# A two-attention block on one Trainium2 core: scores lead by 19 instead of 21, later projections, and instruction lists written anew

## The reference, cut to what matters

```python
# 1: attention with 16 heads of 16; only the 307 rows with the largest
#    sparsity = max(scores) - mean(scores) keep their output, others give zero
scores = einsum('bhqd,bhkd->bhqk', q, k) * scale
sparsity = scores.max(-1) - scores.mean(-1)
_, top_idx = top_k(sparsity, U)                # U = 307 of 512, per head
out_sel = einsum('bhuk,bhkd->bhud', softmax(scores of top_idx), v)
x = x + out.at[..., top_idx].set(out_sel) @ Wo + bo
x = x + ffn(layernorm(x))     # 2: 256 -> 1024 -> 256, 4 of 16 blocks of 64 kept per row by a router
x = x + gla(layernorm(x))     # 3: gated linear attention over the batch axis (8 steps), then a silu ffn
x = x + ffn(layernorm(x))     # 4: the same weights as 2
```

## Time and profile before

| what | value |
|---|---|
| median of 3 runs | 1562.42 us (1561.67 to 1566.0) |
| the profiled execution | 1563.17 us |
| its span | 1561.4 us |
| granted PE clock, mean over the span | 0.977 of full speed |
| front, before unit 0's first T | 0 to 56.4 us |
| 16 units of attention, to the mask | 56.4 to 526 us |
| START | about 530 to 951 us |
| MERGED, then CLOSE | 951 to 1409, then to 1561 us |

### The profile page before, as it was taken

How to read it: one execution, slowest core, us unless ns; L and a number is a source line. 1 busy time by engine, 2 the same in 40 slices (tenths; PEclk the granted TensorE clock), 3 DMA queues, 4 the chain that set the end, 5 groups by cost and what they waited for, 6 DMA issues and landing times.

```text
span 1561.4 us, 25522 instructions
## 1 busy us (share of the span) xinstructions
PE 1473.3 (94%) x8840; PEld 1049.0 (67%) x8840; DVE 1111.0 (71%) x2127; ACT 664.9 (43%) x971; POOL 557.6 (36%) x705
## 2 busy tenths in 40 slices
...
DMA packets 56414, 61.04 MB, mean 39 GB/s; under 512 B 15733, under 2 KB 41637, under 8 KB 56349
## 3 DMA queue, kind: packets, MB, share of 16 engines
...
## 4 chain that ended last, share of the span: by engine, by line
PE 53%; issue 19%; DVE 13%; POOL 8%; ACT 4%; SPq 1%; DMA 1%; POOLq 0%; ACTq 0%; DVEq 0%
PE ps L1961 15%; PE ps L1989 10%; PE ps L958 5%; PE ps L943 4%; PE ps L929 4%; PE ps L886 3%; POOL h L1564 3%; DVE mc L630 2%; PE ps L1972 2%; POOL kT L1537 2%; PE ps L1947 2%; PE ps L896 1%; PE ps L2001 1%; DVE race L729 1%; DVE top L728 1%
## 5 line engine op out<-in xcount | busy, mean ns | idle before, releaser
L630 DVE TENSOR_REDUCE mc<-ps 128x2 f32<-128x1024 f32 x256 | 305.5, 1220 | 46.2 <-PE ps L929 45.7
L1989 PE MATMUL ps<-w_hi,h 128*128 128x256 f32 x1024 | 220.7, 299 | 6.0 <-DVE h L1801 6.0
L1868 ACT ACTIVATE h<-ps 128x512 fp32r<-128x512 f32 x128 | 75.8, 597 | 314.0 <-PE ps L2019 314.0
L1801 DVE SCALAR_TENSOR_TENSOR h<-ps,h 128x512 fp32r<-128x512 f32 x128 | 87.6, 690 | 128.7 <-ACT h L1868 126.0
L346 POOL DMA_DIRECT2D k_st<-k_hi x256 | 124.1, 491 | 152.7 <-PE ps L943 75.3
L1989 PEld LDWEIGHTS ps<-w_hi,h 128*128 128x128 f32 x1024 | 166.9, 190 | 13.7 <-DVE h L1801 11.2
L1961 PE MATMUL ps<-xT_b,w_hi 128*128 128x512 f32 x512 | 166.8, 407 | 0.0
L1564 POOL TENSOR_TENSOR h<-hf,h 128x512 fp32r<-128x512 f32 x56 | 72.5, 1294 | 250.5 <-DVE h L1814 250.5
L1989 PE MATMUL ps<-w_lo,h 128*128 128x256 f32 x512 | 143.9, 281 | 0.0
L943 PE MATMUL ps<-q_st,k_st 64*128 64x512 f32 x512 | 122.7, 478 | 16.6 <-ACT pT1b L816 5.0
L1537 POOL TENSOR_TENSOR kT<-kT,aT 128x128 f32<-128x128 f32 (+6 forms) x56 | 72.0, 1286 | 156.4 <-DVE pr L1728 106.6
...
## 6 DMA issues: line engine op xcount, KB each, us to landing
q_st<-q_hi SPq DMA_DIRECT2D x256, 32.0 KB, 2.1
k_st<-k_hi POOLq DMA_DIRECT2D x256, 32.0 KB, 1.9
q_st<-q_lo SPq DMA_DIRECT2D x128, 32.0 KB, 2.0
k_st<-k_lo POOLq DMA_DIRECT2D x128, 32.0 KB, 1.9
...
```

Of the source, the lines that this page charges most:

```text
L630: v.tensor_reduce(mc[par][:, qt, 2 * HU + j:MC:NPAIR], ps[:, at:at + 2, :], AX_X, ALU.max).then_inc(max_done, 1)
L1801: v.scalar_tensor_tensor(lo[:, :], ps[:, RING[s] + m % 2, :], 0.0, hi[:, :].bitcast(F32), ALU.max, ALU.subtract).then_inc(F[s]["hl"], 1)
L1868: a.activation(h[s][m % 2][0][:, :], ps[:, RING[s] + m % 2, :], ACT.Relu).then_inc(F[s]["relu"], 1)
L1989: last = t_.matmul(ps[:, ACC[s] + t // 2, (t % 2) * D:(t % 2 + 1) * D], h[s][m % 2][a][:, t * P:(t + 1) * P], ws[k][:, m, :], start=m == 0 ...
```

## The change

`AHEAD` goes from 5 to 3: 16 + 3 = 19 scores are made before unit 0, S 0 to 12 of a unit belong to the next unit and S 13 to 15 to the one after. 14 hand-written lists of attention are written anew (those for units 0, odd, even and 14 on PE, ACT and DVE, for unit 15 on PE and ACT). POOL's once-only work goes behind even units only. `START`, `MERGED` and `CLOSE` are written anew. No instruction is added to any engine, and none is removed; they are moved.

```diff
-AHEAD = 5
+AHEAD = 3
 PE_UNITS (the odd and the even list, and the start of unit 14's)
-    "odd": [("S", 0), ("T", 0, 0), ("V0",), ("T", 0, 1), ("S", 1), ("AV", 0), ("T", 1, 0), ("S", 2), ("K", 0),
-        ("S", 3), ("T", 1, 1), ("AV", 1), ("S", 4), ("T", 2, 0), ("K", 1), ("S", 5), ("T", 2, 1), ("S", 6), ("AV", 2),
-        ("T", 3, 0), ("Q", 0), ("Q", 1), ("T", 3, 1), ("S", 7), ("AV", 3), ("S", 8), ("T", 4, 0), ("V1",),
-        ("T", 4, 1), ("S", 9), ("AV", 4), ("T", 5, 0), ("S", 10), ("O1",), ("S", 11), ("T", 5, 1), ("AV", 5), ("mx",),
-        ("T", 6, 0), ("S", 12), ("mean",), ("T", 6, 1), ("S", 13), ("AV", 6), ("T", 7, 0), ("S", 14), ("AV", 7),
-        ("T", 7, 1), ("S", 15), ("O0",)],
+    "odd": [("S", 0), ("S", 1), ("T", 0, 0), ("V0",), ("T", 0, 1), ("AV", 0), ("S", 2), ("S", 3), ("T", 1, 0),
+        ("K", 0), ("K", 1), ("S", 4), ("T", 1, 1), ("S", 5), ("AV", 1), ("T", 2, 0), ("AV", 2), ("S", 6), ("T", 2, 1),
+        ("Q", 0), ("S", 7), ("T", 3, 0), ("S", 8), ("Q", 1), ("S", 9), ("T", 3, 1), ("AV", 3), ("S", 10), ("T", 4, 0),
+        ("V1",), ("T", 4, 1), ("S", 11), ("AV", 4), ("T", 5, 0), ("S", 12), ("O1",), ("S", 13), ("T", 5, 1),
+        ("AV", 5), ("mx",), ("T", 6, 0), ("S", 14), ("AV", 6), ("T", 6, 1), ("mean",), ("S", 15), ("T", 7, 0),
+        ("AV", 7), ("O0",), ("T", 7, 1)],
-    "even": [("S", 0), ("T", 0, 0), ("X0",), ("AV", 0), ("T", 0, 1), ("X1",), ("S", 1), ("T", 1, 0), ("S", 2),
-        ("AV", 1), ("S", 3), ("T", 1, 1), ("K", 0), ("S", 4), ("T", 2, 0), ("K", 1), ("S", 5), ("T", 2, 1), ("AV", 2),
...
+    "even": [("S", 0), ("X0",), ("S", 1), ("T", 0, 0), ("S", 2), ("X1",), ("S", 3), ("T", 0, 1), ("S", 4), ("AV", 0),
+        ("T", 1, 0), ("S", 5), ("AV", 1), ("T", 1, 1), ("S", 6), ("K", 0), ("T", 2, 0), ("K", 1), ("S", 7),
+        ("T", 2, 1), ("S", 8), ("AV", 2), ("T", 3, 0), ("Q", 0), ("Q", 1), ("T", 3, 1), ("AV", 3), ("S", 9),
+        ("T", 4, 0), ("S", 10), ("AV", 4), ("T", 4, 1), ("S", 11), ("O1",), ("S", 12), ("T", 5, 0), ("T", 5, 1),
+        ("mx",), ("AV", 5), ("T", 6, 0), ("S", 13), ("mean",), ("T", 6, 1), ("S", 14), ("AV", 6), ("T", 7, 0),
+        ("S", 15), ("AV", 7), ("T", 7, 1), ("O0",)],
...
 DVE_UNITS (odd)
-    "odd": [("stats", 0), ("max", 0), ("V0",), ("max", 1), ("max", 2), ("stats", 1), ("max", 3), ("max", 4), ("K",),
...
+    "odd": [("stats", 0), ("max", 0), ("max", 1), ("stats", 1), ("V0",), ("max", 2), ("max", 3), ("max", 4),
...
 attention.pool, the loop over units
             unit(u)
-            if u < len(ffn_pieces):
-                ffn_low(u)
-            elif u < len(ffn_pieces) + 3:
-                spread(u - len(ffn_pieces))
-            elif u < len(ffn_pieces) + 6:
+            if u % 2 == 0 and u < 10:
+                ffn_low(u // 2)
+            if u in (2, 4, 6, 8):
+                eng.wait_ge(ffn_lo, u // 2 + 1)
+            if u in (2, 4, 6):
+                spread(u // 2 - 1)
+            if u in (8, 10, 12):
                 eng.wait_ge(v_moved, u // 2 + 1)
-                bias_part(u - len(ffn_pieces) - 3)
+                bias_part((u - 8) // 2)
```

In even units DVE's `x_low` steps move from behind maxima 0 and 1 to behind maximum 4. In unit 14 the maxima are 0 to 12 where they were 0 to 10. In `START`, as PE sees it, the steps around the first two recurrences become:

```diff
-z.T f1.m1c f1.mk z.o0 z.o1 z.o2 og z.o3 z.o4 f1.m0 z.o5 z.o6 z.o7 z.o8 rec0 f1.m1 rec1 f1.d0 rec2 rec3 rec4 rec5 f1.m2 f1.d1 rec6 rec7
+z.T f1.rt z.o0 z.o1 z.o2 og z.o3 z.o4 z.o5 z.o6 z.o7 f1.m0c z.o8 rec0 f1.m1c f1.mk rec1 rec2 rec3 f1.m0 rec4 f1.m1 f1.d0 rec5 f1.m2 rec6 f1.d1 rec7
-g.u1 z.o7 z.o8 rec0 rec1 g.d0 rec2 rec3 rec4 g.m2 rec5 rec6 g.u2 g.d1 rec7 g.m3 g.u3 o.mean
+g.u1 z.o7 z.o8 g.d0 g.m2 rec0 rec1 g.u2 rec2 g.d1 rec3 rec4 g.m3 rec5 rec6 g.u3 g.d2 rec7 g.m4 g.u4 o.mean
```

More of the change, by code:

```diff
@@ L86 @@
 PE_UNITS = {
[18 rows of a table removed]
[L105 removed]
[4 rows of a table removed]
[L110 to L112 removed]
[18 rows of a table added]
+    2 * B - 2: [("S", 0), ("S", 1), ("T", 0, 0), ("S", 2), ("T", 0, 1), ("S", 3), ("S", 4), ("AV", 0), ("S", 5),
[4 rows of a table added]
@@ L114 @@
+    2 * B - 1: [("T", 0, 0), ("T", 0, 1), ("AV", 0), ("T", 1, 0), ("O1",), ("T", 1, 1), ("T", 2, 0), ("T", 2, 1),
+        ("AV", 1), ("T", 3, 0), ("AV", 2), ("AV", 3), ("T", 3, 1), ("T", 4, 0), ("T", 4, 1), ("AV", 4), ("T", 5, 0),
+        ("T", 5, 1), ("T", 6, 0), ("AV", 5), ("O0",), ("T", 6, 1), ("AV", 6), ("AV", 7)]}
 ACT_UNITS = {
-    0: [("X0",), ("exp", 0, 0), ("X1",), ("exp", 0, 1), ("exp", 1, 0), ("exp", 1, 1), ("K",), ("exp", 2, 0),
+    0: [("X0",), ("exp", 0, 0), ("X1",), ("exp", 0, 1), ("exp", 1, 0), ("exp", 1, 1), ("exp", 2, 0), ("K",),
+        ("exp", 2, 1), ("exp", 3, 0), ("exp", 3, 1), ("Q",), ("exp", 4, 0), ("out", 1), ("exp", 4, 1), ("exp", 5, 0),
+        ("exp", 5, 1), ("mx",), ("exp", 6, 0), ("exp", 6, 1), ("exp", 7, 0), ("mean",), ("exp", 7, 1), ("O0",)],
@@ L116 @@
+    "odd": [("out", 0), ("exp", 0, 0), ("exp", 0, 1), ("exp", 1, 0), ("exp", 1, 1), ("K",), ("exp", 2, 0),
         ("exp", 2, 1), ("exp", 3, 0), ("Q",), ("exp", 3, 1), ("exp", 4, 0), ("out", 1), ("exp", 4, 1), ("exp", 5, 0),
[L117 to L121, removed]
@@ L122 @@
-    "even": [("out", 0), ("exp", 0, 0), ("X0",), ("exp", 0, 1), ("X1",), ("exp", 1, 0), ("exp", 1, 1), ("exp", 2, 0),
-        ("K",), ("exp", 2, 1), ("exp", 3, 0), ("Q",), ("exp", 3, 1), ("out", 1), ("exp", 4, 0), ("O1",),
-        ("exp", 4, 1), ("exp", 5, 0), ("exp", 5, 1), ("mx",), ("exp", 6, 0), ("exp", 6, 1), ("mean",), ("exp", 7, 0),
+        ("O1",), ("exp", 5, 1), ("mx",), ("exp", 6, 0), ("exp", 6, 1), ("mean",), ("exp", 7, 0), ("O0",),
+        ("exp", 7, 1)],
+    "even": [("X0",), ("exp", 0, 0), ("out", 0), ("exp", 0, 1), ("X1",), ("exp", 1, 0), ("exp", 1, 1), ("exp", 2, 0),
+        ("K",), ("exp", 2, 1), ("exp", 3, 0), ("Q",), ("exp", 3, 1), ("out", 1), ("exp", 4, 0), ("exp", 4, 1),
+        ("O1",), ("exp", 5, 0), ("exp", 5, 1), ("mx",), ("exp", 6, 0), ("exp", 6, 1), ("mean",), ("exp", 7, 0),
@@ L125 @@
         ("exp", 7, 1), ("O0",)],
     2 * B - 2: [("exp", 0, 0), ("out", 0), ("exp", 0, 1), ("exp", 1, 0), ("exp", 1, 1), ("exp", 2, 0), ("exp", 2, 1),
[L127 to L131, removed]
@@ L133 @@
-DVE_UNITS = {
-    0: [("max", 0), ("max", 1), ("X0",), ("max", 2), ("X1",), ("max", 3), ("K",), ("max", 4), ("max", 5), ("max", 6),
-        ("Q",), ("max", 7), ("max", 8), ("max", 9), ("max", 10), ("max", 11), ("max", 12), ("max", 13), ("max", 14),
-        ("max", 15)],
-    "odd": [("stats", 0), ("max", 0), ("V0",), ("max", 1), ("max", 2), ("stats", 1), ("max", 3), ("max", 4), ("K",),
[L138 to L142, removed]
+        ("O1",), ("mx",), ("exp", 3, 0), ("exp", 3, 1), ("exp", 4, 0), ("out", 1), ("exp", 4, 1), ("exp", 5, 0),
@@ new lines @@
+        ("exp", 5, 1), ("exp", 6, 0), ("exp", 6, 1), ("exp", 7, 0), ("O0",), ("exp", 7, 1)],
+    2 * B - 1: [("out", 0), ("exp", 0, 0), ("exp", 0, 1), ("exp", 1, 0), ("exp", 1, 1), ("O1",), ("exp", 2, 0),
+        ("exp", 2, 1), ("exp", 3, 0), ("exp", 3, 1), ("exp", 4, 0), ("out", 1), ("exp", 4, 1), ("exp", 5, 0),
+        ("exp", 5, 1), ("O0",), ("exp", 6, 0), ("exp", 6, 1)]}
+DVE_UNITS = {
+    0: [("max", 0), ("max", 1), ("max", 2), ("X0",), ("max", 3), ("X1",), ("max", 4), ("max", 5), ("max", 6),
+        ("max", 7), ("K",), ("max", 8), ("Q",), ("max", 9), ("max", 10), ("max", 11), ("max", 12), ("max", 13),
+        ("max", 14), ("max", 15)],
+    "odd": [("stats", 0), ("max", 0), ("max", 1), ("stats", 1), ("V0",), ("max", 2), ("max", 3), ("max", 4),
+        ("max", 5), ("K",), ("max", 6), ("max", 7), ("max", 8), ("Q",), ("max", 9), ("max", 10), ("stats", 2),
+        ("V1",), ("max", 11), ("max", 12), ("stats", 3), ("max", 13), ("max", 14), ("shares",), ("max", 15)],
+    "even": [("max", 0), ("max", 1), ("max", 2), ("max", 3), ("max", 4), ("X0",), ("X1",), ("max", 5), ("max", 6),
+        ("K",), ("max", 7), ("max", 8), ("Q",), ("max", 9), ("max", 10), ("max", 11), ("max", 12), ("max", 13),
+        ("shares",), ("max", 14), ("max", 15)],
@@ L143 @@
     2 * B - 2: [("max", 0), ("max", 1), ("max", 2), ("max", 3), ("max", 4), ("max", 5), ("max", 6), ("max", 7),
-        ("max", 8), ("max", 9), ("max", 10), ("shares",), ("choose", 0, 2), ("choose", 2, 4)],
+        ("max", 8), ("max", 9), ("max", 10), ("max", 11), ("max", 12), ("shares",), ("choose", 0, 2),
+        ("choose", 2, 4)],
     2 * B - 1: [("choose", 4, 7), ("choose", 7, 10), ("choose", 10, 13), ("choose", 13, 16), ("choose", 16, 19),
@@ L1151 @@
 W_STREAM.insert(W_STREAM.index("g.u1") + 1, "o.x")
-START = ["p0.mask", "p1.mask", "p0.T", "p1.T", "p0.wo", "init0", "p1.wo", "p0.x", "f0.ln", "f0.T", "f0.rt",
[31 rows of a table removed]
+START = ["p0.mask", "p1.mask", "p0.T", "p1.T", "p0.wo", "p1.wo", "init0", "p0.x", "f0.ln", "f0.T", "f0.rt",
[31 rows of a table added]
 def counted(names):
```

8 lines of the change are left out of this document (4 added, 4 removed), and 110 rows, old and new, of tables (CLOSE, MERGED, PE_UNITS, START).

## The result

Slower, where faster was forecast. The changed kernel takes 1572.41 us (median of 6 runs, 1570.76 to 1575.73), the kernel before 1563.26 beside it (6 runs): ratio 1.0056, interval 1.0044 to 1.0068. It lies 22 us above the forecast and outside its range. The profiled execution took 1575.73 us, the slowest of the six, with a span of 1573.8 (before 1563.17 and 1561.4), so differences of the two profiles (12.3 us) are larger than that of the medians (9.2).

What follows compares the result with a forecast made beforehand. PE, busy 94% of the span, was taken as the bound, so only its idle time or lowered clock could be won. Terms summed to -12.1 us: 1563.2 to 1551.1, median 1550.3, stated 1550; range 1541 to 1562.

Steps and rivals of the forecast that it cites:

- Once-only works: Attention units 2 to 5: moving POOL's pieces away from x_low makes each unit 28.26 us, -11.0 us; 0 if the collision stays.
- New unit lists: Attention units: longer steps +1.6 us, and more maxima due before mx in odd units +2.8 us.
- max(1.65, PE's work): Attention lists: each step costs the greater of 1.65 us and its PE work; +0.25 us a pair of units, +1.6.
- The thin cover of DVE at mx: Odd units: 13 maxima, not 11, due before mx; +0.4 us for each of 7 units, +2.8, bounds 0 and 10.
- Rival 2: Odd units: DVE late for mx, PE idles and its clock falls; 1567 us, or 1569 with even units; chance 0.08.
- Front: Before unit 0: two scores fewer, made in the shadow of the maxima's DMA; gain 0.3 us, at most 2.3.
- End of attention: Unit 14: 13 maxima instead of 11, so DVE's run ends one maximum later; +1.3 us (0 to +3.5).
- START: First two recurrences: PE work fills idle time beside the POOL and DVE chain; -5.0 us, bounds 0 and -10.
- rival 3: Block part: a POOL and DVE chain sets the idle time, so -6.5 us are not had; 1556.5 us, chance 0.14.
- MERGED: MERGED loop: recurrence steps 5 and 6 one FFN block sooner, inputs ready in time; 0 us, bounds -5.5 and +1 x 5.
- a turn of 92.5: MERGED: a turn above 92.5 us, against 91.6 now, would show a wait at f1.d5 and the forecast wrong.
- CLOSE: CLOSE: g.d6, about 1.4 us, put ahead of e.gT, which waited 3.48 us; -1.5 us (0 to -3.5).

Runs made afterwards that it cites:

- experiment 1: Kernel before, with only POOL's once-only works moved behind the even units: 1554.47 us, ratio 0.9926 to the kernel before.
- experiments 2: Kernel before, with AHEAD = 3 and the new unit lists only, once-only works and block lists as before: ratio 1.0049 to the kernel before.
- 4: Changed kernel with MERGED of the kernel before: ratio 1.0032 to the kernel before.
- experiment 5: Changed kernel with only the end of a MERGED turn, from rec5 on, as before: 1569.72 us, ratio 1.0050 to the kernel before.
- experiment 7: Changed kernel with AV 5 put between the two T 5 of the even units: ratio 1.0011 to the kernel before.
- experiment 11: Changed kernel with units 14 and 15 in the old order, S 11, S 12 and their maxima added: ratio 1.0056 to the kernel before.
- 12: Changed kernel with the once-only works placed as before, all lists as changed: ratio 1.0075 to the kernel before.
- 3: Kernel before, with only START, MERGED and CLOSE of the changed kernel: ratio 1.0018 to the kernel before.
- experiment 13: Changed kernel with AV 5 between even units' two T 5, old MERGED and CLOSE, 4 and 12 unread matmuls in the front: 1560.89 us, ratio 0.9966.
- experiment 15: Kernel before, with once-only works behind even units, changed START, two unread matmuls behind each of scores 16 to 20: 1554.64 us, ratio 0.9955.
- experiment 6: Changed kernel with AHEAD = 5 in place of 3, every list as changed: 1631.52 us, ratio 1.0439 to the kernel before.

## Why the prediction was wrong, point by point

The forecast was -12.1 us and the kernel made +8.8 (0.0056 of 1565), 21 apart. Two groups of terms hold nearly all of it: 12 in lead and unit lists, 9 in the block part.

*Once-only works, -11.0.* Right: -11.6 alone, and in the changed kernel units 2 to 5 are 9.9 us shorter. Only the credit was wrong. The new lists move `x_low` as well, and that alone clears units 2 and 4. So the single experiments don't add: the works and the lists alone make -11.6 and +7.7, with +2.8 for the block part the sum is -1, and the whole made +8.8, because both first edits remove the one stall. In my sum the stall was counted once, and this term did not cause the miss.

*New unit lists, +1.6 and +2.8.* This is the step that failed. With the works moved in both, the changed kernel stands (1.0056 - 0.9926) x 1565 = 20.3 us above experiment 1. The block part takes 2.8 of that, so lead and unit lists cost 17.5; my terms for them, with front and end of attention, were 1.6 + 2.8 - 0.3 + 1.3 = 5.4. The profiled executions differ by 17.7 up to the last exponential (changed less experiment 1): first exponential 1.9, units 0 and 1 6.1, six even units 6.3, six odd units 1.7, units 14 and 15 1.6. In units 0 to 13 alone that is 14.1 against my 4.4. Units 0 and 1 vary between executions: in six other kernels with the same lists and front there (experiments 2, 4, 5, 7, 11, 12), unit 2 begins at 118.1 to 123.6 us, in those with the old ones (before, 1 and 3) at 114.8 to 115.9.
 - My step of max(1.65, PE's work) had no term for TensorE's clock. The bare T 5, T 5 does take what I costed, 1.62 us (257.85 to 259.47). But PE idles for 1.12 of them, and behind that the clock falls, in three of six even units, 1.5 us each. With AV 5 in between (experiment 7) the even units are 28.0 us, 0.1 above experiment 1's: 5.7 us less in the six, 7.0 in the whole.
 - The same holds in units 0 and 1. They take 64.6 us together in the changed kernel and 59.0 in experiment 13, where the clock never falls (unread matmuls hold it in the front): 5.6 us less. The old lists take 58.4 (experiment 1) and, with the clock of the front better kept, 57.3 (experiment 15), so the new order itself costs 0.6 to 1.7.
 - Before that fall at 92.7 us PE waits for the maxima's rows of unit 1. I called Q's later stacks harmless, and they are not later against mx than before. What I did not ask is how many T are left between mx and T 7,0 to cover the rows' way: three before, two now.
 - The thin cover of DVE at mx, +2.8, was not it: odd units are 28.6 to 29.5 us (before 28.3 to 28.9), and PE waits for DVE at mx in unit 0 alone, 0.65 us. Rival 2 had the right means, an idle PE whose clock falls, and the wrong place: behind ACT in even units, not behind DVE in odd ones.

*Front, -0.3.* The first T is released by the DMA of the maxima, as said, now with a wait of 2.94 us, since fewer scores stand ahead of it: the two were in its shadow. The first exponential is at 58.28 us, 1.0 later than before, but the six kernels named above have it at 56.3 to 59.0, and those with the old front at 56.3 to 57.4. So a loss by the front's order is not shown. PE waits 0.87 us for a stack of K before mx, and the clock falls there; experiment 5 has 0.82 there and the first exponential at 56.29, so that wait isn't shown to be the cause either.

*End of attention, +1.3.* By the last exponential it measures +1.6 against experiment 1. The block part waits for the mask, though, and from unit 14's first exponential to the mask's end are 64.2 us, against 62.2 in experiment 1 and 60.9 before; over all kernels 63.1 to 65.5 with lead 19 and 60.9 to 62.2 with the old lists. So the size is about 2 us, inside the bounds. With lead 21 under the new lists it is 62.3 (experiment 6) and with lead 19 in the old order 64.6 (experiment 11), so the two maxima more are the likely cause. They do not follow at once, as I had it, but wait twice for PE, 1.61 us at 472.36 and 0.71 at 479.01.

*START, -5.0.* Nothing that shows. From the mask's start to POOL's first `x` of MERGED are 443.4 us, 444.1 before; all kernels with the new START have 442.7 to 446.6 and all with the old one 443.7 to 445.2. The idle time was moved, not filled (21.9 against 21.1 us), as rival 3 had it: PE's waits at the sums over head channels went from 11.8 to 7.6 us, those for the low part `h` at the second matrices from 1.8 to 3.7, those at the transposes (L1950) from 2.6 to 5.1.

*MERGED, 0.* +3.6 (5 x 0.73). I found DVE's low part of f1.m5 "done just when f1.d5 wants it". It is up to 0.7 us late, and just in time was no room to cost at nothing. The mark that I set, a turn of 92.5, was too coarse: 92.04 is 0.73 above before.

*CLOSE, -1.5.* e.gT's wait went from 3.48 to 2.09 us, as forecast, but a wait of 0.87 for POOL's `h` came and the clock was low there for 6.8 us, not 3.4. From the last turn's mark to the end are 228.3 us against 226.1, of which 0.7 are the turn's. Kernels with the old CLOSE have 226.1 to 227.4, those with the new one, less the turn's part, 226.6 to 227.7: the gain is not there, and a loss is not clear of the spread.

So the block part, forecast at -6.5 us, made +2.8 (1.4 to 4.2), of which MERGED has 3.6.

What stays open: why the clock falls behind some of these waits and not behind others of the same length, what would be left of units 0 and 1 with SP's queue free, and what in START's new order makes the new waits.
